# The order around the expert search, the low weight parts and the last rows, in a one-core attention and expert kernel

## What is computed

```python
x = x + _L0_xattn_ref(_layernorm(x), ctx, Wq, bq, Wk, bk, Wv, bv)   # x: 4 x 1024 x 256, ctx: 4 x 64 x 256
x = x + _L0_ffn_ref(_layernorm(x), gate_w, w1, w2)

def _L0_ffn_ref(x, gate_w, w1, w2):                  # 8 experts, w1: 8 x 256 x 1024, w2: 8 x 1024 x 256
    cap = int(2.0 * T / E)                           # 256 tokens for each expert and batch
    probs = softmax(einsum('BTC,CE->BTE', x, gate_w))
    top_p, top_idx = top_k(transpose(probs, (0, 2, 1)), cap)
    xin = take_along_axis(x[:, None], top_idx[..., None], axis=2)
    h = gelu(einsum('BElC,ECH->BElH', xin, w1), approximate=False)
    y = einsum('BElH,EHC->BElC', h, w2) * top_p[..., None]
    return zeros.at[b_idx, top_idx].add(y)
```

## Time and profile before

| What | us |
|---|---|
| median of three runs | 473.53 |
| the profiled execution | 473.02 |
| its span, first to last instruction | 471.3 |
| TensorE busy | 443.5 |
| VectorE busy | 318.1 |
| ScalarE busy | 212.3 |
| GpSimd busy | 204.7 |
| mean granted TensorE clock | 0.958 |

### The profile page before, as it was taken

How to read it: one execution, slowest core, us unless ns; L and a number is a source line. 1 busy time by engine, 2 the same in 40 slices (tenths; PEclk the granted TensorE clock), 3 DMA queues, 4 the chain that set the end, 5 groups by cost and what they waited for, 6 DMA issues and landing times.

```text
span 471.3 us, 8224 instructions
## 1 busy us (share of the span) xinstructions
PE 443.5 (94%) x2586; PEld 374.6 (79%) x2586; DVE 318.1 (67%) x830; ACT 212.3 (45%) x524; POOL 204.7 (43%) x230
## 2 busy tenths in 40 slices
PE   8999455999999999999999999999999999999993
PEld 7877333887888888888888888888888888888993
DVE  4698989797676567656756675667566756674551
ACT  2488994224362445244524452454245424442331
POOL 6544503031835381538154814481448144813342
PEclk9999755799999999999999999999999999999997
DMA  8984862015428150815081408150815081504142
GB/s 275 362 293 163 295 278 105 23 48 184 79 53 224 36 80 23 223 38 76 23 223 41 72 23 223 44 74 19 223 46 74 17 223 46 79 12 46 15 49 30
DMA packets 35671, 52.51 MB, mean 111 GB/s; under 512 B 3009, under 2 KB 28994, under 8 KB 35138
## 3 DMA queue, kind: packets, MB, share of 16 engines
q1 hardware_dynamic: 22946, 34.89, 22.1%
q0 software_dynamic: 12288, 17.08, 21.2%
q10 hardware_dynamic: 416, 0.27, 0.2%
HBM read 35.17 MB, written 16.92 MB: 111 GB/s over the span
## 4 chain that ended last, share of the span: by engine, by line
PE 79%; DVE 2%; DMA 1%; POOLq 0%; POOL 0%; ACT 0%; issue 0%; ACTq 0%; DVEq 0%
PE bank L1054 36%; PE wide L1071 23%; PE wide L1075 12%; PE bank L821 3%; PE wide L1066 2%; PE bank L1029 1%; DMA xg<-xn_rows,gidx 1%; PE bank L1111 1%; PE wide L821 1%; DVE hlo L1516 0%; POOLq L92 0%; POOL out_dram L587 0%; DVE hhi L1514 0%; PE bank L1117 0%; DVE place L1705 0%
## 5 line engine op out<-in xcount | busy, mean ns | idle before, releaser
L1071 PE MATMUL wide<-w2both,hhi 128*128 128x512 f32 x480 | 176.2, 400 | 0.2 <-DVE ysb L1528 0.2
L587 POOL DMA_INDIRECT out_dram<-ysb,sidx x64 | 107.2, 1675 | 107.3 <-DVE ysb L1528 82.2
L759 ACT ACTIVATE hraw<-bank 128x512 f32<-128x512 f32 (+1 forms) x136 | 77.6, 571 | 137.4 <-PE bank L1054 135.8
L1075 PE MATMUL wide<-w2both,hlo 128*128 128x256 f32 x480 | 134.2, 280 | 0.0
L579 POOL DMA_INDIRECT xg<-xn_rows,gidx x64 | 67.8, 1059 | 129.7 <-issue 95.8
L1514 DVE CAST hhi<-hraw 128x512 fp32r<-128x512 f32 (+1 forms) x136 | 57.8, 425 | 75.5 <-ACT hraw L759 75.3
L1071 PEld LDWEIGHTS wide<-w2both,hhi 128*128 128x128 f32 x480 | 90.4, 188 | 20.1 <-DVE hlo L1516 0.6
L1516 DVE TENSOR_TENSOR hlo<-hraw,hhi 128x512 fp32r<-128x512 f32 (+1 forms) x136 | 90.0, 661 | 4.7
L1075 PEld LDWEIGHTS wide<-w2both,hlo 128*128 128x128 f32 x480 | 90.3, 188 | 3.5
L1054 PE MATMUL bank<-xlo,w1hi 128*128 128x512 f32 (+1 forms) x268 | 80.4, 381 | 0.0
L1054 PE MATMUL bank<-xhi,w1lo 128*128 128x512 f32 (+1 forms) x268 | 80.2, 380 | 0.0
(11 more groups left out here) (198 smaller groups left out, 434.4 us busy)
## 6 DMA issues: line engine op xcount, KB each, us to landing
raw<-in_w_dram SPq DMA_DIRECT2D x16, 1024.0 KB, 6.9
xn_rows<-x_all SPq DMA_DIRECT2D x4, 1060.0 KB, 4.2
x_all<-in_x_dram SPq DMA_DIRECT2D x8, 512.0 KB, 10.1
raw<-in_x_turned_dram SPq DMA_DIRECT2D x8, 512.0 KB, 9.2
out_dram<-x_all SPq DMA_DIRECT2D x8, 512.0 KB, 4.8
xg<-xn_rows,gidx POOLq DMA_INDIRECT x64, 2.9
out_dram<-ysb,sidx POOLq DMA_INDIRECT x64, 4.2
ctxT<-in_ctx_turned_dram ACTq DMA_DIRECT2D x1, 256.0 KB, 3.6
```

What stands on the lines that cost most here:

```text
L587: pool.indirect_dma_start(out=out_rows, out_offset=at, in_=ysb[g][:, i, :], in_offset=None, compute_op=ALU.add).then_inc(rows_added, 16)
L759: act.activation(hraw[s % 2][:, 0:width], bank[s % 2][:, 0:width], ACT.Gelu).then_inc(gelu_done, 1)
L1071: return pe.matmul(y[:, 0:2 * C], hhi[s % 4][:, at], w2both[:, j].rearrange("p a d -> p (a d)"), start=(j == 0), stop=(j == HC - 1), skip_ ...
L1075: return pe.matmul(y[:, 0:C], hlo[s % 4][:, at], w2hi[:, j, :], start=False, stop=False, skip_group_check=True)
```

## The change

Five things are changed; no arithmetic is.

1. VectorE begins the search for half 0 between the residuals of groups 5 to 7. `add_late` is cut into `invert_late(g, h)` and `add_late(g, i)`, and the three first rounds hold the residuals of groups 6 and 7 in their gaps. The softmax of half 1 moves behind rounds 3 to 5, and half 1's search starts behind round 6 of half 0 instead of 3. TensorE's counts are in the matching order. ScalarE's `normalise(0)` stands between the squares of group 5 and group 6.
2. GpSimd makes all eight `w1lo` of the first expert ahead of the first gather, and all eight `w2lo` between the first gather and the second. VectorE made these before.
3. Half 1's last rounds, its list and the turning of group 1's rows stand one step later in the first expert (`turn_step` 6, `list_step` 7, `index_step` 8, `next_step` 12; `rank_first(1)` at step 2, `list_first(1)` at step 3, `rank_rest` at step 5). Both turns are made in one place, in the middle of `ff2(6)`, into banks 2 and 3.
4. `raise_floor(1, 8)` and `raise_floor(1, 9)` stand behind an `ff1`, not right behind their counts.
5. `last_rows` covers five steps instead of four, with one more buffer for `hhi` and `hlo`, and leaves four products of the last tile for the end instead of two.

```diff
-        def next_step(e): return 11 if is_first(e) else 10
+        def next_step(e): return 12 if is_first(e) else 10
-        def list_step(e): return 6 if is_first(e) else 3
+        def list_step(e): return 7 if is_first(e) else 3
...
@@ gpsimd
-            for g in range(NU):
-                pool.wait_ge(xn_stored[g], 16 * HB)
-                pool.wait_ge(gidx_ready, g + 1)
-                gather(g, FIRST if g == 0 else 0)
+            pool.wait_ge(own_set, 2 + 2 * B + 3 * HB)
+            for j in range(HC):
+                pool.wait_ge(w1_hi, j + 1)
+                pool.tensor_tensor(w1lo[:, j], w1raw[:, :, bass.ts(j, P)], w1hi[:, j].bitcast(F32),
+                                   ALU.subtract).then_inc(w1_split, 1)
+            pool.wait_ge(xn_stored[0], 16 * HB)
+            pool.wait_ge(gidx_ready, 1)
+            gather(0, FIRST)
+            for j in range(HC):
+                pool.wait_ge(w2_hi, j + 1)
+                pool.tensor_tensor(w2lo[:, j], w2raw[:, j], w2hi[:, j].bitcast(F32), ALU.subtract).then_inc(w2_split, 1)
+            pool.wait_ge(xn_stored[1], 16 * HB)
+            pool.wait_ge(gidx_ready, 2)
+            gather(1)
@@ scalar
             gate_exp(0, HALF, 0)
             copy_turned(NG - 1)
-            for g in range(NG - 3, NG):
-                squares(g)
+            squares(NG - 3)
             act.wait_ge(rows_stored[0], 16 * (NG // 2))
             act.wait_ge(nb2_ready, 1)
             normalise(0)
+            squares(NG - 2)
+            squares(NG - 1)
             gate_exp(HALF, NC, 1)
             normalise(1)
@@ tensor
-            TAIL = 4
+            TAIL = 5
             def last_rows(e, steps):
-                a, b, c, z = range(steps - TAIL, steps)
-                ff1(c, ST * e + c, e, True)
-                ff1(z, ST * e + z, e, True)
-                for s in (a, b, c):
+                o, a, b, c, z = range(steps - TAIL, steps)
+                for s in (b, c, z):
+                    ff1(s, ST * e + s, e, True)
+                for s in (o, a, b, c):
                     pe.wait_ge(h_split, ST * e + s + 1)
                     ff2_tile(s, NL - 2, e, True)
-                for s in (a, b):
-                    ff2_tile(s, NL - 1, e, True)
+                ff2_tile(o, NL - 1, e, True)
                 pe.wait_ge(h_split, ST * e + z + 1)
                 ff2_tile(z, NL - 2, e, True).then_inc(tile_done, 1)
-                for s in (c, z):
+                for s in (a, b, c, z):
                     t = ff2_tile(s, NL - 1, e, True)
@@ tensor, expert
+                    if s == turn_step(e) and is_first(e):
+                        for i in range(NL):
+                            if i == NL // 2:
+                                pe.wait_ge(gathered[1], gathered_rows(1, e))
+                                turn_rows(1, 0, KC)
+                                pe.wait_ge(block_ready, 1)
+                                turn_rows(1, 1, KC, 3)
...
+                            t = ff2_tile(s, i, e, last)
+                        t.then_inc(ff2_done, 1)
...
+                    if s in (0, 1) and is_first(e):
+                        raise_floor(1, 8 + s)
...
+                    if s == 0 and is_first(e):
+                        count(1, 0, 9)
+                        count(1, 1, 9)
@@ vector
+            residual(mid, 0)
             sum_probs(0, HALF, 0)
+            residual(mid, 1)
             invert_sum(0, HALF, 0)
...
             first_half(0)
+            invert_late(late, 1)
+            add_late(late, 2)
+            keep_reached(0, 0)
+            add_late(late, 3)
+
+            first_half(1)
+            invert_late(end, 0)
+            add_late(end, 0)
+            keep_reached(0, 1)
+            add_late(end, 1)
...
+            first_half(4)
             dve.wait_ge(rstd2, 5)
             scale_logits(HALF, NC, 1)
...
@@ vector, expert
                     if s == 1 and is_first(e):
+                        place_rows(1)
+                        place_masked(1)
+                        slot_rows(1)
+                        block_rows(1)
+                        token_rows(1)
+                    if s == 2 and is_first(e):
                         own_rows(1)
                         index_rows(1)
+                    if s == 3 and is_first(e):
                         mark_rest()
-                    if s == 2 and is_first(e):
                         sum_rest()
```

More of the change, by code:

```diff
@@ L205, in build @@
         hraw = [sb(f"hraw{i}", [P, UT], F32) for i in range(2)]
-        hhi = [sb(f"hhi{i}", [P, UT], F32R) for i in range(4)]
-        hlo = [sb(f"hlo{i}", [P, UT], F32R) for i in range(4)]
+        hhi = [sb(f"hhi{i}", [P, UT if i < 4 else UT // 2], F32R) for i in range(5)]
+        hlo = [sb(f"hlo{i}", [P, UT if i < 4 else UT // 2], F32R) for i in range(5)]
         kv_loaded = sem("kv_loaded")
@@ L389, in part, with h_at @@
             return s // HC, s % HC, slice(0, UT), UT
+        def h_at(s, last):
+            return 4 if last and s == steps_of(last) - 1 else s % 4
         def joined(g, last):
@@ L704, in gate_exp @@
                 act.activation(pr, pr, ACT.Exp).then_inc(gexp, 1)
-            gate_exp(0, HALF, 0)
-            copy_turned(NG - 1)
-            for g in range(NG - 3, NG):
-                squares(g)
             def normalise(g):
@@ L720, in keep_probabilities @@
                                half(prob, h).rearrange("p b c e -> p (b c) e"), ACT.Copy).then_inc(xn2_ready, 1)
+            gate_exp(0, HALF, 0)
+            copy_turned(NG - 1)
+            squares(NG - 3)
             act.wait_ge(rows_stored[0], 16 * (NG // 2))
@@ L786, in expert @@
                 for s in range(steps_of(last)):
-                    if s in (turn_step(e), turn_step(e) + 1):
+                    if s == turn_step(e) and is_first(e):
+                        for k in range(KC):
+                            x_part(1, k, 3 + k, 2 + k)
+                    if s in (turn_step(e), turn_step(e) + 1) and not is_first(e):
                         k = s - turn_step(e)
@@ L994, in list_first @@
                 t.then_inc(first_listed, 1)
-            for n in range(3):
+            for n in range(6):
                 first_half(n)
-            both_counted(3, 0)
-            both_raised(4, 0)
+            count(0, 0, 6)
+            count(0, 1, 6)
+            count(1, 0, 0)
+            raise_floor(0, 6)
+            count(1, 1, 0)
+            both_raised(7, 0)
             count(1, 0, 1)
+            count(0, 0, 8)
+            count(0, 1, 8)
             count(1, 1, 1)
-            both_raised(5, 1)
-            both_counted(6, 2)
-            both_raised(7, 2)
-            both_counted(8, 3)
-            both_raised(9, 3)
-            count(1, 0, 4)
+            raise_floor(0, 8)
+            both_raised(9, 1)
+            count(1, 0, 2)
+            count(1, 1, 2)
             rank_first(0)
-            count(1, 1, 4)
-            raise_floor(1, 4)
+            raise_floor(1, 2)
+            count(1, 0, 3)
             list_first(0)
-            for n in range(5, 8):
-                second_half(n)
-                if n < 7:
-                    keep_warm(bank[4], 3)
+            count(1, 1, 3)
+            raise_floor(1, 3)
+            second_half(4)
+            keep_warm(bank[4], 3)
+            second_half(5)
+            keep_warm(bank[4], 3)
+            second_half(6)
             def rank_rest():
@@ L1065, in ff2_tile @@
                     for m, (hh, w) in enumerate(((hhi, w2hi), (hhi, w2lo), (hlo, w2hi))):
-                        t = pe.matmul(y[:, 0:C], hh[s % 4][:, at], w[:, j, :], start=(j == 0 and m == 0),
+                        t = pe.matmul(y[:, 0:C], hh[h_at(s, last)][:, at], w[:, j, :], start=(j == 0 and m == 0),
                                       stop=(j == HC - 1 and m == 2), skip_group_check=True)
@@ L1070, in by_hi @@
                 def by_hi():
-                    return pe.matmul(y[:, 0:2 * C], hhi[s % 4][:, at], w2both[:, j].rearrange("p a d -> p (a d)"),
+                    return pe.matmul(y[:, 0:2 * C], hhi[h_at(s, last)][:, at], w2both[:, j].rearrange("p a d -> p (a d)"),
                                      start=(j == 0), stop=(j == HC - 1), skip_group_check=True)
                 def by_lo():
-                    return pe.matmul(y[:, 0:C], hlo[s % 4][:, at], w2hi[:, j, :], start=False, stop=False,
+                    return pe.matmul(y[:, 0:C], hlo[h_at(s, last)][:, at], w2hi[:, j, :], start=False, stop=False,
                                      skip_group_check=True)
@@ L1133, in _ @@
             first_low(1, False)
-            raise_floor(1, 8)
+            raise_floor(1, 7)
             pe.wait_ge(x_hi, KC)
@@ L1656, in _ @@
             first_rest(1, False)
-            for j in range(3):
-                w2_rest(j, j)
-            keep_reached(1, 8)
-            w1_rest(6, 6)
+            keep_reached(1, 7)
             first_rest(0, True)
@@ L1663, in _ @@
             dve.sem_inc(y_ready, NL)
```

(5 more changed lines are left out.)

206 lines of the change are left out of this document (94 added, 112 removed).

## The result

The changed kernel takes 477.53 us (median; 477.02 to 478.17), the kernel before, on the same chip, 473.60 us (median). The ratio is 1.0074, with a 95% interval of 1.005 to 1.0098: 3.5 us slower, from 2.4 to 4.6. The forecast was 476.4 us, with 62% for slower. The profiled execution spans 476.1 us where before's spanned 471.3, 4.8 more.

| stretch | before, us | after, us | measured | forecast |
|---|---|---|---|---|
| start to the first transposes | 82.73 | 85.55 | +2.82 | +1.6 |
| transposes to `ff2(8)` | 34.49 | 37.05 | +2.56 | +2.0 |
| `ff2(8)` to the last matmul's end | 346.77 | 346.92 | +0.15 | 0 |
| last matmul's end to the end | 7.31 | 6.58 | -0.73 | -0.7 |

A forecast was written before the change was run, and what follows sets the result against it. TensorE, busy 94% of the span, was taken to bound the kernel, leaving its start, waits before 120 us and the tail. +1.6 + 2.0 - 0.7 = +2.9 us gave 476.4 on the median; range 474.6 to 478.3, with rivals 471.6 to 479.5.

The forecast's parts named there:

- The search's start: VectorE's first comparison at 49.35 us, 4.0 us sooner; the first list about 3.0 us sooner, near 74.1 us.
- ScalarE's delay: Second half's logits scaled at 57.7 us instead of 54.91, so ScalarE's `w1hi` starts 2.8 us later, at 73.9 us.
- The first term: First gather waits in GpSimd's queue behind eight `w1lo` at 0.60 us each, starting at 79.7 us: +1.6 us.
- Rival C: GpSimd and VectorE hold each other up; the eight subtractions take 7.2 us instead of 4.8: +5.3, 478.8 us; 15%.
- The second term: Second list a step later delays second gather and next expert's weights; TensorE waits about 2.2 us at `ff2(8)`: +2.0 us.
- The tail: Third term: four part-products instead of two behind tile 2's last one, so the end comes sooner: -0.7 us.
- D: Subtractions keep ScalarE's pace, gather 1.0 us sooner, second list's lateness covered: -1.8, about 471.7 us; needs under 0.45 us each; 20%.
- E: Subtractions at ScalarE's pace, but the weights' wait as computed: +0.3, 473.8 us; 6%.
- Rival B: The weights' wait doesn't come, the load being quicker than 8.0 us with the gathers out of its way: +0.7, 474.2 us; 12%.

The follow-up runs named there:

- pool_only: The kernel before, changed only so that GpSimd makes `w1lo` ahead of the first gather and `w2lo` behind it: 479.09 us, ratio 1.0113.
- load_free: The changed kernel, with Sync not waiting for the gather of group 1 before it loads the second expert's weights: 476.39 us, ratio 1.0055 to the kernel before.
- none_first: The changed kernel, with GpSimd making all eight `w1lo` behind the first gather, ahead of the `w2lo`: 473.99 us, ratio 1.000 to the kernel before.
- turns_ahead: low_on_dve_free with TensorE's `rank_rest` a step sooner and its first transposes ahead of `raise_floor(1, 6)`: 471.48 us, ratio 0.9963 to the kernel before.
- low_on_dve_free: The changed kernel, first expert's low parts back on VectorE, Sync not waiting for the second gather before loading the second expert's weights: 472.69 us, ratio 0.9972.

## Why the prediction was right, and where it was not

**The search's start and ScalarE's delay** came as forecast: 49.41 against 49.35, the list at 74.04 against 74.1, `w1hi` at 74.12 against 73.9. For the second half's logits, 57.92 against 57.7, luck helped: the first round was taken at 1.69 us and took 2.12, and 0.91 us was taken from the fifth pair of comparisons to the logits, which took 0.61. VectorE also had eight reciprocals to do there, not the six that I counted; no term used that number.

**The first term** had its mechanism right and its size wrong. "I take 0.60 us, next to the iota" was the step: measured are 0.78 us beside VectorE's comparisons and 0.69 us mostly without, against the upper end of 0.79 us. That is 1.44 us more for eight. Two smaller things went back: 0.18 us from the last subtraction to the gather instead of 0.6, and a landing 0.18 us quicker. The first subtraction started at 74.67 and not at 74.3, 0.37 us late, of which 0.22 is `w1hi`'s. So 1.6 + 1.44 + 0.37 - 0.42 - 0.18 = 2.81, against 2.82 measured. The iota matched in size but has no input; the iota and the small two-input operation together, which I had as the upper end, came near. The Trainium skill's figure (GPSIMD Engine Reference, section 3.1), scaled, had given an estimate of about 0.75 us and +2.8; the trace agrees with it.

**Rival C** had 15%, for subtractions drawn out to 0.9 us. The hold-up is real and goes both ways: a subtraction takes 0.73 to 0.86 us beside comparisons instead of 0.69, and a comparison up to 0.94 us instead of 0.38, and once, in pool_only, 5.43. The Trainium skill, SBUF — State Buffer, "Who interferes with whom", says that a VectorE instruction with two SBUF inputs contends with a GpSimd instruction that reads SBUF, and the traces agree. An instruction with one input took longer here too (a `key` of 128x128 0.64 us at 77.93 while GpSimd subtracted, 0.21 at 76.86 in the kernel before). In the changed kernel this fell on rounds of the second half behind which TensorE waited 2.63 us for the gather anyway; pool_only shows what it costs where somebody waits.

**The second term** was +2.56 against +2.0. The chain from gather to weights sets the end of the stretch, as forecast, and was later within the forecast's bounds: the second gather moved from 16.41 to 18.93 us behind the transposes, 2.52 and not 2.0, and ScalarE's first `w1hi` by 2.56. The 0.5 us more was there before the gather: TensorE was through with the second list 17.55 us behind the transposes, where 99.6 - 82.73 = 16.87 was taken. By then it had lost 0.6 us to the clock and 0.34 to ScalarE's `hraw`, which the sum put at nothing. And TensorE did not run up to `ff2(8)` and wait 2.2 us there. With another 0.72 us lost to `place_rest` on the way it waited only 0.93. The step that failed is "TensorE reaches `ff2(8)` at the same time as before, 116.9": I followed the list that moved and not `rank_rest`, which moved with it. So two causes lie one behind the other. load_free takes the weights' part away: the kernel is 0.9 us quicker by the ratios and 1.3 in the spans, and half of the stretch's loss stays. The failed step did not move the number only because the weights came later still. No run put the second list back to step 2 by itself, so what that step costs is read from the rows.

**The tail** was right, -0.73 and -0.65 in two kernels' traces.

The forecast of 476.4 lay 1.1 us under the time. Rivals D (faster, 20%) and E failed by their own condition: a subtraction takes 0.69 us at best, not under 0.45. Rival B failed too: the weights' wait came, 0.93 us of it.

## What to carry to other kernels

Work that is moved to an idle engine costs what stands behind it in that engine's queue: the eight `w1lo` ahead of the gather lost 3.5 us (none_first against the change), the eight `w2lo` behind it gained 1.7. Before work is given to GpSimd, look at what VectorE does in the same microseconds and whether anybody waits for that; and look for a neighbour row with the same number of inputs, not only of the same size. Where an early issue doesn't bring an early landing, read the DMA share of that window. When a wait is taken away, read it too: the same line guarded one order and held up the other.

## What the runs showed of the chip that was not expected

- GpSimd's subtraction of 128x256 float32 takes 0.69 us (7 in 4.83), beside VectorE's comparisons 0.73 to 0.86 (5.84 and 6.24 for 8, 6.05 for 7).
- VectorE's comparison of 128x448 int16 takes 0.38 us alone and 0.91 to 0.93 beside it, a pair 0.69 and 1.2 to 1.77. One comparison, in pool_only, took 5.43 us and ended 0.24 us behind a run of seven subtractions.
- Gathers issued while the DMA engines were half busy (share 0.49 and 0.52) were waited for to 6.5 and 6.3 us behind their issue (none_first, turns_ahead), on idle engines to 4.4 to 4.6 (pool_only, load_free, the change, before).
- After the first transposes the clock rose at 4.6 us before and at 5.7 us after. In the changed kernel TensorE had been idle for 2.63 us ahead of them, before for 0.51. The idle time alone does not order the kernels: in load_free it was 2.60 us and the clock rose at 5.3, in turns_ahead 1.37 and 3.2, in low_on_dve_free none and 4.3.
